# Two-level convolution kernel: the halves of a 1x1 made one behind the other, each in its bank, and one identity group moved behind them

## The reference, cut to what matters

```python
# layer 0, input x (8, 64, 128, 128), after a group norm; ATT = 16
for i in range(4):                         # level i
    y = x if i == 0 else mean over blocks of 2**i x 2**i
    d = 1 if i == 0 else 2 * (i + 1) + 1
    y = relu(conv3x3(y, ds_w3[i], ds_b3[i], pad=d, dil=d))
    feats.append(conv1x1(y, ds_w1[i], ds_b1[i]))
def att(t):
    f_att, f_idt = t[:, :16], t[:, 16:]
    ker = (gelu(f_att.mean(axis=(2, 3)) @ kg_w1.T + kg_b1) @ kg_w2.T + kg_b2)   # a 3x3 filter per image
    out = conv13x13(f_att, lk_filter) + depthwise3x3(f_att, ker)
    return conv1x1(concatenate([out, f_idt]), fus_w, fus_b)
x = x + conv1x1(att(feats[0]) + sum of upsampled att(feats[i]), fin_w, fin_b)
# layer 1: x = x + (a 5x5 and a folded 3x3 convolution of the group norm of x)
```

## Time and profile before

| what | value |
|---|---|
| median of 3 runs | 2959.62 us |
| the profiled execution's own time | 2955.59 us |
| its span, first to last instruction | 2953.6 us |
| TensorE (PE) busy | 2657.0 us, 90% |
| VectorE (DVE) busy | 2159.9 us, 73% |
| ScalarE (ACT) busy | 1050.4 us, 36% |
| GpSimd (POOL) busy | 619.9 us, 21% |
| mean granted TensorE clock | 0.935 |
| first matmul of level 1 / last of its large filters' outputs | 52.9 us / about 677 us |

### The profile page before, as it was taken

How to read it: one execution, slowest core, us unless ns; L and a number is a source line. 1 busy time by engine, 2 the same in 40 slices (tenths; PEclk the granted TensorE clock), 3 DMA queues, 4 the chain that set the end, 5 groups by cost and what they waited for, 6 DMA issues and landing times. The chain is left out here.

```text
span 2953.6 us, 39022 instructions
## 1 busy us (share of the span) xinstructions
PE 2657.0 (90%) x12262; PEld 2136.0 (72%) x12262; DVE 2159.9 (73%) x2987; ACT 1050.4 (36%) x1621; POOL 619.9 (21%) x660
## 2 busy tenths in 40 slices
PE   3899999985999699999999598899975999999998
PEld 3677777764888588888888477777754777777776
DVE  4544444453555588888888889989886999999998
ACT  1111111100100298898998322222202333323332
POOL 5444443412220334434434100000001000000000
PEclk9899999987888699999999799999987999999999
DMA  6222222211000699999997224433352423333332
GB/s 127 48 70 71 69 71 73 73 30 38 13 13 8 110 213 219 217 211 221 219 216 182 107 88 157 149 131 132 120 185 94 121 90 107 104 95 116 91 118 60
DMA packets 288702, 338.04 MB, mean 114 GB/s; under 512 B 24816, under 2 KB 243824, under 8 KB 274288
## 3 DMA queue, kind: packets, MB, share of 16 engines
q1 hardware_dynamic: 277184, 332.76, 41.7%
q10 hardware_dynamic: 11440, 4.28, 0.8%
HBM read 211.60 MB, written 122.62 MB: 113 GB/s over the span
## 5 line engine op out<-in xcount | busy, mean ns | idle before, releaser
L167 PE MATMUL ps_all<-vh,u_h 128*128 128x512 f32 x960 | 385.2, 401 | 29.2 <-DVE vl L2742 28.2
L169 PE MATMUL ps_all<-vh,u_l 128*128 128x512 f32 x960 | 383.3, 399 | 0.0
L168 PE MATMUL ps_all<-vl,u_h 128*128 128x512 f32 x960 | 382.7, 399 | 0.0
L2651 ACT ACTIVATE vh<-rt,gn 128x528 fp32r<-128x528 f32 x192 | 130.9, 727 | 446.4 <-DVE rt L2719 331.5
L167 PE MATMUL ps_all<-vh,t_h 128*128 128x512 f32 x576 | 231.5, 402 | 23.7 <-DVE vl L1797 23.7
L167 PEld LDWEIGHTS ps_all<-vh,u_h 128*128 128x128 f32 x960 | 180.9, 188 | 83.9 <-issue 38.2
L168 PE MATMUL ps_all<-vl,t_h 128*128 128x512 f32 x576 | 229.6, 399 | 0.0
L169 PE MATMUL ps_all<-vh,t_l 128*128 128x512 f32 x576 | 229.5, 398 | 0.0
L169 PEld LDWEIGHTS ps_all<-vh,u_l 128*128 128x128 f32 x960 | 180.9, 188 | 46.2
L168 PEld LDWEIGHTS ps_all<-vl,u_h 128*128 128x128 f32 x960 | 181.2, 189 | 45.5
L167 PE MATMUL ps_all<-nh,w3h 128*128 128x512 f32 (+1 forms) x396 | 161.0, 407 | 36.5 <-POOL nl L1174 28.0
(11 more groups left out here) (390 smaller groups left out, 6760.4 us busy)
## 6 DMA issues: line engine op xcount, KB each, us to landing
xc<-in_x SPq DMA_DIRECT2D x128, 256.0 KB, 3.9
xr<-in_x SPq DMA_DIRECT2D x128, 256.0 KB, 4.2
x_layer<-xr SPq DMA_DIRECT2D x64, 512.0 KB, 2.7
xq<-x_layer SPq DMA_DIRECT2D x32, 1024.0 KB, 4.9
x_layer<-xq SPq DMA_DIRECT2D x32, 1024.0 KB, 3.9
out<-ot SPq DMA_DIRECT2D x64, 512.0 KB, 5.1
xw<-in_x SPq DMA_DIRECT2D x112, 288.0 KB, 5.0
xw<-x_layer SPq DMA_DIRECT2D x16, 1152.0 KB, 8.8
```

The lines of the kernel that those rows point to most:

```text
L167: pe.matmul(o, wh, xh, start=first, stop=False, skip_group_check=True)
L168: pe.matmul(o, wh, xl, start=False, stop=False, skip_group_check=True)
L169: return pe.matmul(o, wl, xh, start=False, stop=last, skip_group_check=True)
L2651: act.activation(vh[:, v % 2, n, :, :].rearrange("p a b -> p (a b)"), rt[:, n, :, :].rearrange("p a b -> p (a b)"), ACT.Identity, scale=gn ...
```

## The change

Three things change in level 1, in all eight images.

- The 1x1 is written with the half outside and the pixel class inside: 24 matmuls of half 0, then 24 of half 1. Half 0 goes to `ps_stat`, half 1 to the first bank of `ps_q`, each with a wait of its own.
- Identity group 2 is made behind the 1x1 rather than before it, and its copy by VectorE stands behind the pooled values instead of before the subtractions.
- Which bank a group uses, and how many groups must be out before it may begin, stand in the tables `BANK` and `USED`; `ORDER_OF` gives the place of an identity group among the ten.

```diff
-            QF, QL, QY = 3, 5, 6
+            QF, QY = 2, 6
+            ORDER_OF = {0: 0, 1: 1, 2: 4, 3: 5}
+            BANK = {0: ps_q[:, 0, :], 1: ps_q[:, 1, :], 2: ps_stat, 3: ps_q[:, 0, :], 4: ps_q[:, 1, :], 5: ps_q[:, 0, :],
+                    6: ps_q[:, 1, :], 7: ps_q[:, 0, :], 8: ps_q[:, 1, :], 9: ps_q[:, 0, :]}
+            USED = {0: 0, 1: 0, 2: 0, 3: 1, 4: 2, 5: 4, 6: 5, 7: 6, 8: 7, 9: 8}
...
# VectorE
-                        for k in range(3):
+                        for k in range(2):
                             plain(i, k)
...
                         chain_pooled_dve(dve, i, ((1, 1),), pooled_s, chain)
+                        plain(i, 2)
...
# TensorE
-                        u = k if k < 3 else QL
+                        u = ORDER_OF[k]
                         pe.wait_ge(r_l, 2 + NCH * i + k + 1)
-                        pe.wait_ge(qfree, Q * i + u + 1)
+                        pe.wait_ge(qfree, 2 + Q * i + USED[u])
...
-                        for k in range(3):
+                        for k in range(2):
                             plain(i, k)
...
-                        pe.wait_ge(qfree, Q * i + QF + 2)
-                        for j, (dr, dc) in enumerate(PIX):
-                            a = 112 - ATT * slot(dr, dc)
-                            for hf in range(2):
+                        for hf in range(2):
+                            pe.wait_ge(qfree, 2 + Q * i + USED[QF + hf])
+                            for j, (dr, dc) in enumerate(PIX):
+                                a = 112 - ATT * slot(dr, dc)
                                 v = (slice(hf * C, hf * C + C), slice(dr, None, 2), slice(dc, dc + 4 * NQ1 + 5, 4))
                                 w = (v[0], 0, slice(a, a + P))
-                                mm = product(pe, ps_q[:, 1 - hf, 0:NB1 * (NQ1 + 2)].rearrange("p (n q) -> p n q", q=NQ1 + 2),
+                                mm = product(pe, BANK[QF + hf][:, 0:NB1 * (NQ1 + 2)].rearrange("p (n q) -> p n q", q=NQ1 + 2),
                                              fa_h[w], fa_l[w], rh[v], rl[v], j == 0, j == 7)
-                                if j == 7:
-                                    mm.then_inc(qful, 1)
-                        pe.wait_ge(qfree, 2 + Q * i + QL)
+                            mm.then_inc(qful, 1)
+                        plain(i, 2)
+                        pe.wait_ge(qfree, 2 + Q * i + QF + 2)
                         pe.wait_ge(l_l, i + 1)
```

More of the change, by code:

```diff
@@ L610, in body @@
                             p0 = 3 + NB1 * hf
-                            ps = ps_q[:, 1 - hf, 0:NB1 * (NQ1 + 2)].rearrange("p (n q) -> p n q", q=NQ1 + 2)
+                            ps = BANK[QF + hf][:, 0:NB1 * (NQ1 + 2)].rearrange("p (n q) -> p n q", q=NQ1 + 2)
                             for hp, c0 in inner:
@@ L693, in plain @@
                     def plain(i, k):
-                        u = k if k < 3 else QL
+                        u = ORDER_OF[k]
                         dve.wait_ge(qful, Q * i + u + 1)
                         dve.tensor_copy(z1[:, 8 * k:8 * k + 8, :].rearrange("p a b -> p (a b)"),
-                                        ps_q[:, u % 2, :]).then_inc(qfree, 1)
+                                        BANK[u]).then_inc(qfree, 1)
                     def split_w3(k):
@@ L899, in body @@
                             v = z1[:, dr::2, :].rearrange("p n (q s) -> p n q s", s=4)[:, :, :, dc:dc + 2]
-                            dve.tensor_tensor(v, v, ps_q[:, p % 2, :].rearrange("p (s n q) -> p n q s", s=2, q=NQ1),
+                            dve.tensor_tensor(v, v, BANK[QY + p].rearrange("p (s n q) -> p n q s", s=2, q=NQ1),
                                               ALU.add).then_inc(qfree, 1)
@@ L938, in plain @@
                     def plain(i, k):
-                        u = k if k < 3 else QL
+                        u = ORDER_OF[k]
                         pe.wait_ge(r_l, 2 + NCH * i + k + 1)
-                        pe.wait_ge(qfree, Q * i + u + 1)
+                        pe.wait_ge(qfree, 2 + Q * i + USED[u])
                         v = (slice(None), slice(8 * k, 8 * k + 8), slice(2, 2 + S1))
-                        product(pe, ps_q[:, u % 2, :].rearrange("p (r c) -> p r c", c=S1), idt_h[:, 0, :],
+                        product(pe, BANK[u].rearrange("p (r c) -> p r c", c=S1), idt_h[:, 0, :],
                                 idt_l[:, 0, :], rh[v], rl[v], True, True).then_inc(qful, 1)
@@ L996, in body @@
                         for p in range(4):
-                            pe.wait_ge(qfree, Q * i + QY + p + 1)
+                            pe.wait_ge(qfree, 2 + Q * i + USED[QY + p])
                             for e in range(2):
                                 dr, dc = PIX[2 * p + e]
-                                o = ps_q[:, p % 2, e * NB1 * NQ1:(e + 1) * NB1 * NQ1]
+                                o = BANK[QY + p][:, e * NB1 * NQ1:(e + 1) * NB1 * NQ1]
                                 for hf in range(2):
```

## The result

The change makes the kernel slower, as forecast. The median is 2983.86 us (four runs, 2982.67 to 2985.68) against 2961.25 us for the kernel before (four runs, 2959.27 to 2965.05): ratio 1.0073, 95% interval 1.006 to 1.0085. The forecast was 2978.9 us, 5.0 us less, in a range of 2946 to 2996.

What follows compares the result with a forecast made beforehand. TensorE was busy 90% of the span, level 1 a chain of TensorE stages with short waits; 37.6 - 10.4 - 7.9 = +19.3 us on 2959.6 gave 2978.9 us, range 2946 to 2996.

Steps and rivals of the forecast that it cites:

- The 1x1 stage: Level 1's 1x1: halves one behind the other, (48 - 3) x 0.243 = 10.9 us instead of 6.24, +37.6 us over eight images.
- The start: Before the 1x1: with the third identity group moved away, the 1x1 begins earlier, -10.4 us over eight images.
- The way out: Between 1x1 and large filter: only one half's activations and subtractions remain behind the last matmul, -7.9 us.
- The clock: TensorE's granted clock in the large filter: taken as 0, between -11.3 us (low level all back) and +3.6.
- VectorE's copy, queues and later banks: The identity group's copy (0.69 us) behind the pooled values, the queues and later banks: nothing is late, all at nothing.
- The sum: Whole kernel: 37.6 - 10.4 - 7.9 = +19.3 us.
- TensorE looks further ahead: Rival in the 1x1: reach over all 24 keeps halves side by side, only -10.4 us, 2949.2 us; chance 0.18.
- The stepped read is slow only because both halves read: Rival in the 1x1: a half alone goes at 0.13 us, all gains stay, -18.3, 2941.3 us; chance 0.04.
- A weight load cannot lie beside a matmul of the same rows: Rival in the 1x1: 48 unhidden loads of about 0.11 us, +5.3 us an image, 3021 us; chance 0.06.

Runs made afterwards that it cites:

- e_pairs: Changed kernel with pixel class outside and half inside again, so halves alternate after every class: 2951.93 us, ratio 0.9972 against the kernel before.
- e_block2: Changed kernel with halves alternating every two pixel classes (six matmuls each), one wait for both banks ahead: 2955.85 us, ratio 0.998 against the kernel before.
- e_block4: Changed kernel with halves alternating every four pixel classes (12 matmuls each), one wait for both banks ahead: 2982.78 us in one run.
- e_onewait: Changed kernel with the second half's wait for its bank moved ahead of both halves, 24 matmuls then 24: 2990.79 us in one run.
- e_seq_only: Changed kernel with the third identity group back ahead of the 1x1, halves still one behind the other: 2990.29 us, ratio 1.0099 against the kernel before.
- e_pairs_stay: Changed kernel with halves alternating after every class and the third identity group back before the 1x1: 2962.09 us, ratio 1.0003 against the kernel before.
- e_contig_seq: Changed kernel with the 1x1 reading neighbouring columns instead of every fourth, computing other values than the reference: 2976.94 us in one run.

## Why the prediction was right, point by point

- **The 1x1 stage** (+37.6 forecast, +42.7 measured) is the term that was mis-sized, and the step of it that failed is the price of a lone matmul: 0.243 us, scaled from layer 0's 272-column rows, where 0.259 was measured. Over 44 steps and eight images that is 5.6 us, about the whole distance between 19.3 and the 24.6 us of level 1. The pair's own pace of 0.26 us stood beside it in the earlier trace rows and was the exact number: e_pairs and the change share it, so a half without its partner costs what the pair cost. The scaled price took one distance for the whole of a stepped read. The next rows (kernel before, timeline) suggest that it has a part in the distance behind it, too:

```profile
1207.74 0.29 PE L167 MATMUL ps_all<-rp_h,fa_h 128*128 128x272 f32 x1
1207.87 0.41 PE L168 MATMUL ps_all<-rl,fa_h 128*128 128x272 f32 x1
```

From 1207.36 to 1207.74 one stepped and one contiguous matmul take 0.38 us; a contiguous one takes 0.13 (to 1207.87). That leaves 0.25 for the stepped one, and 0.25 x 288/272 = 0.26 us (an estimate). The count of steps was right: three matmuls overlap where the halves meet, and e_block2, e_block4 and e_onewait show three under every order of blocks tried.

- **The start** (-10.4, measured -11.8): right in mechanism, with -1.1 to -1.4 us in images 1, 3, 4 and 5 for -0.95, -0.7 in images 2 and 6 for -0.5, and -2.9 and -2.7 in images 0 and 7 for -2.8. The 1x1 of image 4 follows `rl` by 0.18 us, where 0.36 was forecast: the pooled product and the turn take 0.13 us, not 0.3. What was called the third identity group's departure is two parts: e_seq_only still wins 5.9 us without moving it, by the new bank, and the move adds 5.9.
- **The way out** (-7.9, measured -8.1): one half's activations and subtractions, as forecast. The identity group lay in the wait and cost nothing.
- **The clock** (0, between -11.3 and +3.6; measured +1.8 for the large filter): the choice of 0 came out close, and partly by luck, since with other edits of the same place the filters differ from those of before by -1.4 us (e_seq_only) to +8.2 (e_block4). Over their first 6.5 us, which the term was about, the wait ahead fell from 3.08 to 0.51 us (image 4) without bringing anything back: the granted clock is 0.64 in the mean of the eight images, 0.67 before. The 1x1 itself now runs at 1.2 GHz for most of its time, but that it hands its clock on is not shown. In e_pairs_stay's image 4 a 1x1 at 1.00 stands before a filter at 0.53; in e_block2's image 0 a 1x1 at 0.67 before a filter at 1.00. The upper bound was too low for such edits: in e_pairs the same filter took 6.2 us more.
- **VectorE's copy, queues and later banks** at nothing: in images 1 to 6 nothing in the large filter beyond its clock is left for them (29.57 us at 0.92 in image 4, on the line that the other kernels give). In image 7, where the wait for VectorE is 1.35 us longer than before, e_pairs has the same copy and a wait of 2.36 us, so the copy does not make it.
- **The sum**: +19.3 forecast, +24.6 in level 1 of the two profiles (5.1 too little for the 1x1 and 1.8 for the clock, against 1.6 too little for the two gains), +22.6 between the medians.

The rivals. *TensorE looks further ahead* is refuted with one wait as with two. *The stepped read is slow only because both halves read* is refuted by the first rows of the 1x1, 0.26 us apart with 64 partitions reading, and by the contiguous kernels, where the step alone is changed. *A weight load cannot lie beside a matmul of the same rows* is refuted by the same rows (not 0.35 us) and more sharply by e_contig_seq: 0.15 us from start to start with a weight load of the same 64 rows recorded as 0.19 us in each:

```profile
402.61 0.19 PEld L167 LDWEIGHTS ps_all<-rh,fa_h 64*128 64x128 f32 x1
402.75 0.19 PEld L168 LDWEIGHTS ps_all<-rl,fa_h 64*128 64x128 f32 x1
```

The Trainium skill, "TensorE: Matmul & The Clock Gate", Part 3, says in its list of what overlaps that a load overlaps a matmul only in another row group, and that matmuls keep to the order of the program in start and end. The traces agree with neither: the loads above lie beside matmuls of their own rows, and the second half's first matmul starts ahead of three that precede it.

What stays open is where the low spells of the clock fall. The runs put a price on a microsecond of them, and show that they moved with each edit tried; no run tells what would remove them from a kernel that computes the reference.

## What to carry to other kernels

Before two half-width streams that stand alternately in the program are put one behind the other, look at whether they run in company: x2 rows with equal starts mean that a pair is paid as one, and the separation costs as many steps as it removes partners. Here 42.7 us were paid to shorten two waits worth 20. What was good in the change did not need it: a spare bank and a group moved behind the critical stage, with the halves left in pairs, gave 0.28% (e_pairs). And for a lone matmul, take the pace from the operation's own rows before one scaled from another shape.

## What was not expected of the hardware

- At every junction TensorE starts a matmul of the other 64 rows ahead of exactly three that precede it, with or without a wait between, and at 0.24 us a step (e_contig_seq) as at 0.26. Each matmul here has a weight load of its own and the halves write to different banks; whether the reach counts matmuls or instructions, and what it is in one bank, no run tells.
- A 288-column matmul with a step of four elements of four bytes takes 0.259 us at 2.4 and at 1.2 GHz, with 64 partitions reading or twice 64; contiguous it takes 0.15 and 0.24. So at the low clock the step costs almost nothing. The Trainium skill, "SBUF — State Buffer", Door 1, says that each access to a new line of 16 bytes pays a penalty; the traces agree as far as a step of 16 bytes costs 0.11 us per 288 columns at 2.4 GHz, but no run tries another step, so that the line is the cause is not shown.
- A stretch of lone halves without any idle time can run at 1.2 GHz: 96.50 to 104.40 us in image 0 of the change has TensorE busy all through, at 0.50:

```profile
96.50:104.40 7.90, 7.90 (x36) 7.90 (x34) 0.97 (x2) 0.96 (x2) 7.25 (x9) 0.50 0.00 0
```
